# A decoder block: the first head's probabilities turned by the DMA queues and VectorE in place of TensorE

## The chip, the cores and the metric

The kernel runs on one NeuronCore of a Trainium2 chip. The metric is the device time of one execution in microseconds (us); the median of three runs before the change is 3028.91 us (3027.8 to 3032.17).

## The reference, cut to what matters

Sixteen sequences (B = 16) of 512 tokens of width 512 pass four phases: linear attention with a local convolution (A), cross-attention to `ctx_1024` (B), a recurrent gate over the sequence of items (C), and an output layer (D). The change is in B. There each of 4 heads has 128 dimensions and all heads share one key and one value head:

```
q = rope(rmsnorm(x) @ q_w)              # 4 heads, 512 tokens, 128
k, v = rope(mem @ k_w), mem @ v_w       # one head, 512 keys
logits = q @ k.T                        # 4 x 512 x 512
probs = softmax(where(mask, logits, -big))
enc = probs @ v ; out = enc @ out_w
```

All matrix products are made of three passes over operands that are split in a high part (fp32r, rounded) and a low part (the remainder), so that they keep nearly fp32 precision.

## The kernel before, in words

**Pipeline.** In phase B `pipeline3` runs 18 steps s. A step works on three items at once: `new` (item s: keys, values, queries), `old` (item s-1: softmax and the first three heads' products) and `fin` (item s-2: last head and output). Each step has 16 slots j = 0..15, one per softmax tile (head h = j // 4, 128 tokens t = j % 4, all 512 keys). Each engine walks the slots in its own written order and waits on semaphores; nothing is planned at run time. SyncE (SP) issues every DMA, strictly in its written order: a wait of one DMA holds all later ones.

**The life of a softmax tile.** On TensorE `logits(j)` writes one of two PSUM banks. On VectorE `masked(j)` adds the mask row, takes the maximum and writes the tile to `soft`, which has 4 places (so tile j+4 waits until tile j has been read). ScalarE takes `exp`, VectorE `one_over`, GpSimd `normalise` (L1316). TensorE turns the tile, `turn_p(j)` (L1723): four fp32 transposes of 128x128 into one of two banks. ScalarE's `p_high` (L1388) and VectorE's `p_low` (L1539) split the turned tile into `p[h % 2]`; `turn_p(j)` waits for `p_low(j-2)`, since the bank is the same. `encode(h)` multiplies the four turned tiles of a head with v. In slot j an engine works on: logits(j+2), turn_p(j) on TensorE; one_over(j+1), masked(j+2), p_low(j-1) on VectorE, in this order; p_high(j-1), exp(j+2) on ScalarE; normalise(j+1) on GpSimd. `encode(0)` of `old` is in slot 8.

**Other work in the slots.** TensorE: values and keys of `new` in slots 0, 2, 3, the output of `fin` in 4 to 7, the queries of `new` in 9 to 14. VectorE: `tokens_turned(c)`, a transpose in 32x32 squares of the x of `new` (L388), in slots 5 to 8, and `residual` beside it. ScalarE: `tokens_high(c)` (L1416) in 5 to 8 and `memory_high(c)` (L1243), the split of the next item's memory, in 6 to 9; both stand ahead of the next slot's p_high in ScalarE's order. GpSimd: `tokens_low(c)` (L1320) in slots 6 to 8.

**SP's order in a step.** Load the residual of `fin`; `shuffle_x`: wait for the normalised x, store it to DRAM (`out` is used as scratch, L1118), wait until it has landed, and load it back with its 128-column blocks moved (four DMAs of 256 KB in pieces of 512 B, L382); then the next item's mask (L1127), its memory (L1109), its x (L1114), and the store of `fin` (L1302).

Of the kernel before, what the change touches and what calls it, by code (L numbers as in the profile page):

```python
# [7 lines left out]
F32 = mybir.dt.float32  # L8
# [188 lines left out]
class Kernel:  # L197
# [842 lines left out]
    def phase_b(self, ctx):  # L1040
# [5 lines left out]
        SLOTS = 4  # L1046
        with ExitStack() as held:
# [8 lines left out]
            q = self.split(ctx, "b_q", [P, H, S])  # L1056
            p = [self.split(ctx, f"b_p{i}", [P, T, S]) for i in range(2)]
            memT = Split(sb("memT_hi", [P, C, S], F32R), Place(nc, self.base + 1024 * 196).tile("b_memT_lo", [P, C, S], F32R))
# [33 lines left out]
            kv_ps, v_hi, v_lo = ev("kv_ps", 2), ev("v_hi", 2 * T), ev("v_lo", T)  # L1092
            k_rope = ev("k_rope", 8)
            kT_ps, k_hi, k_lo = ev("kT_ps"), ev("k_hi"), ev("k_lo")
            x_moved = ev("x_moved", 5, 16)
            x_turned, xT_hi, xT_lo = ev("x_turned", C), ev("xT_hi", C), ev("xT_lo", C)
            q_ps, q_cos, q_swapped, q_sin, q_rope = ev("q_ps", H), ev("q_cos", H), ev("q_swapped", 2 * H), ev("q_sin", H), ev("q_rope", H)
# [3 lines left out]
            pT_ps, p_hi, p_lo = ev("pT_ps", J), ev("p_hi", J), ev("p_lo", J)  # L1101
# [4 lines left out]
            def load_mem(sp, b):  # L1106
                if b >= 1:
                    sp.wait_ge(kv_ps.sem, kv_ps.upto(b - 1))
                sp.dma_start(memT_f[:, :, :], self.token_rows(self.x2, b)).then_inc(mem_in.sem, mem_in.unit)  # L1109
# [6 lines left out]
            def shuffle_x(sp, b):  # L1116
                sp.wait_ge(N.normed.sem, N.normed.upto(b))
                sp.dma_start(self.token_rows(self.out, b), x[:, :, :]).then_inc(x_moved.sem, x_moved.unit)  # L1118
                sp.wait_ge(x_moved.sem, x_moved.upto(b - 1, 0))
                self.load_shuffled(sp, x, self.out, b, x_moved)  # L1120
# [150 lines left out]

            def sync(sp):
                def step(s, new, old, fin):
                    if fin:
# [13 lines left out]
                    if s == B - 1:  # L1288
                        self.c_parameters(sp)
                        sp.wait_ge(kv_ps.sem, kv_ps.upto(B - 1))  # L1290
# [18 lines left out]
            def gpsimd(pool):  # L1309
                pool.wait_ge(params.sem, params.upto(0))  # L1310

                def step(s, new, old, fin):
# [8 lines left out]

                    def query_sin(b, h):
# [9 lines left out]
                    for j in range(J):  # L1332
                        if old and j < J - 1:
                            normalise(old.b, j + 1)
                        if new and j == J - 1:
                            normalise(new.b, 0)
                        if older_goes_on:
# [36 lines left out]
            def scalar(act):  # L1374
                def step(s, new, old, fin):
# [6 lines left out]
                    def p_high(b, j):  # L1382
                        h, t = divmod(j, T)
                        act.wait_ge(pT_ps.sem, pT_ps.upto(b, j))
# [3 lines left out]
                        act.activation(p[h % 2].high[:, :, t * P:(t + 1) * P], pT_banks[j % 2][:, :].rearrange("p (i s) -> p i s", i=T),  # L1388
                                       ACT.Copy).then_inc(p_hi.sem, p_hi.unit)

# [6 lines left out]
                    def values_high(g):  # L1397
                        act.wait_ge(kv_ps.sem, kv_ps.upto(new.b, g))
# [12 lines left out]
                    def tokens_high(c):  # L1411
                        act.wait_ge(x_turned.sem, x_turned.upto(new.b, c))
                        source = turns.bank(s, OUT + c)[:, :] if new.b == 0 else nT_f[:, c, :]
                        if c == 0 and new.b >= 1:
                            act.wait_ge(q_ps.sem, q_ps.upto(new.b - 1))
                        act.activation(nT.high[:, c, :], source, ACT.Copy).then_inc(xT_hi.sem, xT_hi.unit)  # L1416

                    def keys_high():
                        act.wait_ge(kT_ps.sem, kT_ps.upto(new.b))
                        if new.b >= 2:  # L1420
                            act.wait_ge(logit_ps.sem, logit_ps.upto(new.b - 2))
                        act.activation(k[new.par].high[:, :], turns.bank(s, KT)[:, :], ACT.Copy).then_inc(k_hi.sem, k_hi.unit)

                    def query_swap(h):

                        act.wait_ge(q_ps.sem, q_ps.upto(new.b, h))
# [13 lines left out]
                    for j in range(J):  # L1440
                        if old and j >= 1:
                            p_high(old.b, j - 1)
                        if fin:
# [69 lines left out]
            def vector(dve):  # L1513
                dve.wait_ge(params.sem, params.upto(0))

                def step(s, new, old, fin):
# [5 lines left out]
                    def masked(b, j):  # L1522
# [3 lines left out]
                        if free := earlier(pT_ps, b, j, SLOTS):  # L1526
# [8 lines left out]
                    def p_low(b, j):  # L1535
                        h, t = divmod(j, T)
                        dve.wait_ge(p_hi.sem, p_hi.upto(b, j))
# [14 lines left out]
                    def tokens_turned(c):  # L1552
                        if c == 0:
                            dve.wait_ge(x_moved.sem, x_moved.upto(new.b - 1))
                            dve.wait_ge(q_ps.sem, q_ps.upto(new.b - 1))
# [10 lines left out]
                    def keys(g):  # L1566
# [8 lines left out]
                        if g == 0 and new.b >= 1:  # L1575
                            dve.wait_ge(kT_ps.sem, kT_ps.upto(new.b - 1))
# [923 lines left out]
```

## Time and profile before

| | |
|---|---|
| median of 3 runs | 3028.91 us |
| the profiled execution itself | 3028.35 us |
| its span | 3026.6 us |
| TensorE (PE) busy | 2983.4 us, 99% |
| VectorE / ScalarE / GpSimd busy | 1952.0 / 1295.3 / 919.5 us |
| DMA, mean share of 16 engines | 43.2% |
| TensorE's granted clock, mean | 0.997 |

Phase B takes about 880 to 1815 us of the span; from one step to the next pass 57.22 us. Busy shares are averages; a row of a timeline gives start, duration, engine, line, operation and how often; the brackets give the idle time just before and what ended it.

### The profile page before, as it was taken

The numbers are of one execution on the slowest core, as the hardware profiler recorded it, in microseconds if no ns is written. First come the engines' busy times: TensorE is split into PE (matmuls) and PEld (weight loads), VectorE is DVE, ScalarE is ACT, GpSimd is POOL, SyncE is SP. The second block draws the span as 40 slices with busy tenths as digits, with TensorE's granted clock in tenths as the row PEclk, the third lists the DMA queues.
The fourth block names the chain that finished last, engine by engine and source line by source line (L and its number), as shares of the span: only waits on it lengthen the run. The fifth ranks groups of instructions, "written<-read, shape, count | busy, mean of one in ns | idle before, by whom it ended". The sixth has DMA issues, their size and how long they took to land.

```text
span 3026.6 us, 39400 instructions
## 1 busy us (share of the span) xinstructions
PE 2983.4 (99%) x14628; PEld 2508.4 (83%) x14628; DVE 1952.0 (64%) x4095; ACT 1295.3 (43%) x2511; POOL 919.5 (30%) x681
## 2 busy tenths in 40 slices
PE   7999999999989999999999999999999999999999
PEld 6888888888868888888888878888888888888887
DVE  6888888888878888888888774323333433232455
ACT  4444444444457766767766643211112212112243
POOL 0101010101357877777777720000000000000144
PEclk9999999999999999999999999999999999999999
DMA  7777777777733334344344232111111121111486
GB/s 212 201 203 209 202 215 199 215 198 217 205 105 113 105 107 127 99 113 127 99 114 126 71 125 74 56 54 55 42 42 42 56 55 57 42 28 46 153 290 224
DMA packets 319631, 380.07 MB, mean 126 GB/s; under 512 B 15312, under 2 KB 175056, under 8 KB 319440
## 3 DMA queue, kind: packets, MB, share of 16 engines
q1 hardware_dynamic: 319440, 377.56, 43.2%
q8 instruction: 116, 1.90, 0.3%
q14 instruction: 75, 0.61, 0.1%
HBM read 232.80 MB, written 130.02 MB: 120 GB/s over the span
## 4 chain that ended last, share of the span: by engine, by line
PE 96%; DVE 2%; ACT 1%; issue 1%; DMA 0%; POOL 0%; SPq 0%; DVEq 0%; ACTq 0%; POOLq 0%
PE c_p L132 11%; PE c_p L131 11%; PE c_p L130 11%; PE a_p L130 6%; PE a_p L131 6%; PE a_p L132 6%; PE b_n L130 5%; PE b_n L132 5%; PE b_n L131 5%; PE b_t L1723 3%; PE d_p L131 2%; PE d_p L132 2%; PE d_p L130 2%; PE a_p L1017 2%; PE a_r L131 2%; PE a_r L132 2%
## 5 line engine op out<-in xcount | busy, mean ns | idle before, releaser
L1316 POOL TENSOR_SCALAR b_soft<-b_soft,b_one_in_sum 128x512 f32<-128x512 f32 x256 | 401.2, 1568 | 201.5 <-DVE b_one_in_sum L1520 201.3
L1997 ACT ACTIVATE c_gate<-c_p,c_bias 128x512 f32<-128x512 f32 x180 | 124.2, 690 | 682.6 <-PE c_p L132 682.6
L2027 DVE TENSOR_TENSOR c_gate<-c_gate,c_gate 128x512 f32<-128x512 f32 x64 | 44.2, 691 | 502.7 <-ACT c_gate L1997 502.7
L351 POOL TENSOR_TENSOR kept_scale<-c_ln_ve,minus_half 128x4 f32<-128x4 f32 x16 | 16.1, 1008 | 880.4 <-DVE c_ln_ve L343 880.4
L1531 DVE CUSTOM_DVE_ANT_0 b_soft<-b_l,b_mask_row 128x512 f32<-128x512 f32 x256 | 175.6, 686 | 87.9 <-issue 84.0
L351 POOL TENSOR_TENSOR a_ln_sc<-a_ln_ve,minus_half 128x4 f32<-128x4 f32 x16 | 16.3, 1017 | 629.9 <-DVE a_ln_ve L343 629.9
L1379 ACT ACTIVATE b_soft<-b_soft,b_minus_top 128x512 f32<-128x512 f32 x256 | 184.5, 721 | 44.6 <-DVE b_minus_top L1531 42.6
L649 ACT ACTIVATE a_elu<-a_p 128x512 f32<-128x512 f32 x128 | 75.6, 591 | 287.6 <-PE a_p L132 287.6
L1388 ACT ACTIVATE b_p_hi<-b_t 128x512 fp32r<-128x512 f32 x256 | 151.3, 591 | 109.9 <-PE b_t L1723 109.6
L1539 DVE TENSOR_TENSOR b_p_lo<-b_t,b_p_hi 128x512 fp32r<-128x512 f32 x256 | 175.7, 686 | 16.1 <-ACT b_p_hi L1388 14.3
L1723 PE MATMUL b_t<-ident,b_soft 128*128 128x128 f32 x1024 | 154.5, 273 | 4.9 <-POOL b_soft L1316 4.9
L2221 POOL TENSOR_TENSOR d_x<-d_x,d_y 128x512 f32<-128x512 f32 x60 | 79.8, 1332 | 252.8 <-ACT d_y L2238 252.8
L1723 PEld LDWEIGHTS b_t<-ident,b_soft 128*128 128x128 f32 x1024 | 126.0, 142 | 30.5 <-DVE b_p_lo L1539 6.4
L130 PE MATMUL b_l<-b_k_hi,b_q_hi 128*128 128x512 f32 x256 | 123.2, 481 | 2.0 <-POOL b_q_lo L1328 1.6
L2029 DVE TENSOR_TENSOR c_gate<-c_gate,c_c_f 128x512 f32<-128x512 f32 x64 | 44.3, 692 | 116.3 <-ACT c_gate L1997 116.3
L130 PE MATMUL a_p<-a_Wk_hi,a_xT_hi 128*128 128x512 f32 x256 | 105.3, 411 | 0.7 <-DVE a_Wk_lo L194 0.7
L626 POOL TENSOR_TENSOR a_res<-a_res,a_bp 128x512 f32<-128x512 f32 x64 | 82.3, 1318 | 75.9 <-DMA a_res<-in_x 47.4
L666 ACT ACTIVATE a_z_hi<-a_z_sum 128x512 fp32r<-128x512 f32 x64 | 40.5, 633 | 150.2 <-DVE a_z_sum L848 150.2
L130 PE MATMUL b_n<-b_nT_hi,b_qw_hi 128*128 128x512 f32 x256 | 100.7, 393 | 3.0 <-POOL b_nT_lo L1320 3.0
L130 PE MATMUL b_e<-b_p_hi,b_v_hi 128*128 128x512 f32 x256 | 100.4, 392 | 2.9 <-DVE b_enc_lo L1544 2.9
L132 PE MATMUL b_l<-b_k_hi,b_q_lo 128*128 128x512 f32 x256 | 102.0, 398 | 0.0
L130 PE MATMUL a_r<-a_Wp_hi,a_z_hi 128*128 128x512 f32 x256 | 101.2, 395 | 0.0
(301 smaller groups left out, 9617.6 us busy)
## 6 DMA issues: line engine op xcount, KB each, us to landing
a_mem_moving<-in_ctx SPq DMA_DIRECT2D x64, 256.0 KB, 5.2
a_mem_turned<-in_ctx SPq DMA_DIRECT2D x16, 1024.0 KB, 9.2
x<-a_mem_turned SPq DMA_DIRECT2D x16, 1024.0 KB, 7.8
a_res<-in_x SPq DMA_DIRECT2D x16, 1024.0 KB, 6.4
x<-a_res SPq DMA_DIRECT2D x16, 1024.0 KB, 5.2
b_memT_f<-x SPq DMA_DIRECT2D x16, 1024.0 KB, 7.3
b_x<-x SPq DMA_DIRECT2D x16, 1024.0 KB, 6.1
b_res<-x SPq DMA_DIRECT2D x16, 1024.0 KB, 5.5
```

What stands on the lines that cost most here:

```text
L130: pe.matmul(out, stationary.high, moving.high, start=first, stop=False)
L131: pe.matmul(out, stationary.high, moving.low, start=False, stop=False)
L132: return pe.matmul(out, stationary.low, moving.high, start=False, stop=last)
L626: pool.tensor_tensor(res[:, t, :], res[:, t, :], bp[:, :], ALU.add).then_inc(res_bp.sem, res_bp.unit)
L1316: pool.tensor_scalar(soft[:, at, :], soft[:, at, :], one_in_sum[:, at:at + 1], None, ALU.mult).then_inc(p_norm.sem, p_norm.unit)
L1379: act.activation(soft[:, at, :], soft[:, at, :], ACT.Exp, bias=minus_top[:, at:at + 1], scale=-1.0, accum_out=row_sum[:, at:at + 1]).then_ ...
L1388: act.activation(p[h % 2].high[:, :, t * P:(t + 1) * P], pT_banks[j % 2][:, :].rearrange("p (i s) -> p i s", i=T), ACT.Copy).then_inc(p_hi ...
L1531: dve.tensor_tensor_reduce(out=soft[:, at, :], in0=logit_banks[j % 2][:, :], in1=mask_row[b % 2][:, :], scale=-1.0, scalar=3e38, op0=ALU.a ...
L1539: dve.tensor_tensor(part.low, pT_banks[j % 2][:, :].rearrange("p (i s) -> p i s", i=T), part.high_f32(), ALU.subtract).then_inc(p_lo.sem, ...
L1723: mm = pe.transpose(pT_banks[j % 2][:, i * P:(i + 1) * P], soft[:, tile(old.b, j), i * P:(i + 1) * P], self.ident[:, :])
L1997: act.activation(gate[j % 2][i][:, :], gating.banks[(3 * j + i) % 6][:, :], ACT.Tanh if g == "c" else ACT.Sigmoid, bias=added[:, i, j:j + ...
L2221: pool.tensor_tensor(x[old.par][:, t, :], x[old.par][:, t, :], y[:, t % 2, :], ALU.add).then_inc(out_sb.sem, out_sb.unit)
```

## The change: what it does

The four tiles of head 0 of each item no longer go through TensorE. `turn_p` runs only for j >= 4. In their place:

- `shuffle_p(t)` on SP: wait for `normalise(t)`; store the `soft` tile (256 KB) to DRAM; wait until it has landed; wait until VectorE has turned tile t-1 (there is one buffer, `p_shuffled`); load it back in four DMAs of 64 KB in pieces of 512 B.
- `first_head_turned(t)` on VectorE in slots 3 to 6, after `masked` and `p_low`: one transpose in 32x32 squares, 128x512, into `p0_raw`.
- `first_head_high(t)` on ScalarE and `first_head_low(t)` on GpSimd in slots 4 to 7: the split of the turned tile, read from SBUF. The `p_high` and `p_low` of head 0 (slots 1 to 4) are gone.
- SP's order in a step is now: residual load, shuffle_p(0), store_x, shuffle_p(1), shuffle_x (its four loads), shuffle_p(2), shuffle_p(3), mask, memory, x, store.
- A place of `soft` that held a tile of head 0 is free once its store has landed (`soft_free`): masked(4) to masked(7) wait for the stores of tiles 0 to 3.
- `encode(0)` waits for GpSimd's four low halves.
- Keys and mask row are kept in another order of columns (key i*128+w in column 4w+i), so that the 32x32 squares come out right. For that `turn_p` of the other 12 tiles reads every fourth column (a step of 16 bytes), and the copies of the keys from PSUM and of the mask read their source in steps of 128 elements.
- Several semaphores are merged into one (`kvq_ps`), with the same order.

```diff
+            def shuffle_p(sp, b, t):
+                rows = self.out[b, t * P:(t + 1) * P, :]
+                sp.wait_ge(p_norm.sem, p_norm.upto(b, t))
+                sp.dma_start(rows, soft[:, t, :]).then_inc(p_moved.sem, p_moved.unit)
+                sp.wait_ge(p_moved.sem, p_moved.upto(b, 5 * t))
+                if b >= 1 or t >= 1:
+                    sp.wait_ge(p_lo.sem, p_lo.upto(b - (t == 0), first_turned_at[t - 1]))
+                for a in range(4):
+                    sp.dma_start(p_shuffled[32 * a:32 * (a + 1), 0, :].rearrange("m (g n) -> m g n", n=P),
+                                 rows[:, a * P:(a + 1) * P].rearrange("(g m) n -> m g n", m=32)).then_inc(p_moved.sem, p_moved.unit)
...
+                    if old:
+                        shuffle_p(sp, old.b, 0)
+                    if new and new.b >= 1:
+                        store_x(sp, new.b)
+                    if old:
+                        shuffle_p(sp, old.b, 1)
                     if new and new.b >= 1:
                         shuffle_x(sp, new.b)
+                    if old:
+                        shuffle_p(sp, old.b, 2)
+                        shuffle_p(sp, old.b, 3)
                     if following(new, B):
                         load_mask(sp, new.b + 1)
                         load_mem(sp, new.b + 1)
...
-                        if free := earlier(pT_ps, b, j, SLOTS):
+                        if free := soft_free(b, j):
                             dve.wait_ge(*free)
...
+                    def first_head_turned(t):
+                        dve.wait_ge(p_moved.sem, p_moved.upto(old.b, 5 * t + 4))
+                        if t == 0 and old.b >= 1:
+                            dve.wait_ge(enc_ps.sem, enc_ps.upto(old.b - 1, 2))
+                        blocks = p_shuffled[:, 0, :].rearrange("p (n i) -> p i n", i=T)
+                        dve.transpose(p0_raw[:, :, t * P:(t + 1) * P], blocks).then_inc(p_lo.sem, p_lo.unit)
...
-                            mm = pe.transpose(pT_banks[j % 2][:, i * P:(i + 1) * P], soft[:, tile(old.b, j), i * P:(i + 1) * P], self.ident[:, :])
+                            mm = pe.transpose(pT_banks[j % 2][:, i * P:(i + 1) * P], interleaved(soft[:, tile(old.b, j), :], i, T), self.ident[:, :])
...
-                        if old:
+                        if old and j >= T:
                             turn_p(j)
```

## Rows read from the trace of the kernel before

**Rows 1.** The page: busy time of the engines, and the chain that ended last.
```profile
PE 2983.4 (99%) x14628; PEld 2508.4 (83%) x14628; DVE 1952.0 (64%) x4095; ACT 1295.3 (43%) x2511; POOL 919.5 (30%) x681
...
PE 96%; DVE 2%; ACT 1%; issue 1%; DMA 0%; POOL 0%; SPq 0%; DVEq 0%; ACTq 0%; POOLq 0%
```

**Rows 2.** The chain in order of time (start, us, piece), one turn of a tile.
```profile
1228.70 0.44 PE b_t L1723 x4
```

**Rows 3.** Turns reading every fourth column: chain 846 to 860; weight loads, min/median/max ns.
```profile
851.36 0.47 PE b_n L369 x4
...
L369 PEld LDWEIGHTS b_n<-ident,b_x x16: 196/210/221, 847.8 to 857.9; 128*128 128x128 f32 x16
...
L1723 PEld LDWEIGHTS b_t<-ident,b_soft x1024: 137/140/230, 880.3 to 1785.7; 128*128 128x128 f32 x171
```

**Rows 4.** TensorE's timeline of one step: logits(2), (5), (8), turn_p(6), encode(0).
```profile
1275.67 0.48 PE L130 MATMUL b_l<-b_k_hi,b_q_hi 128*128 128x512 f32 x1
...
1286.11 0.48 PE L130 MATMUL b_l<-b_k_hi,b_q_hi 128*128 128x512 f32 x1
...
1296.43 0.47 PE L130 MATMUL b_l<-b_k_hi,b_q_hi 128*128 128x512 f32 x1
...
1299.94 0.60 PE L1723 MATMUL b_t<-ident,b_soft 128*128 128x128 f32 x4
...
1305.38 0.40 PE L130 MATMUL b_e<-b_p_hi,b_v_hi 128*128 128x512 f32 x1
```

**Rows 5.** VectorE's timeline of the same step: masked(5), masked(6), p_low(4).
```profile
1287.10 0.69 DVE L1531 CUSTOM_DVE_ANT_0 b_soft<-b_l,b_mask_row 128x512 f32<-128x512 f32 x1 [0.61 <-issue]
...
1290.55 0.69 DVE L1531 CUSTOM_DVE_ANT_0 b_soft<-b_l,b_mask_row 128x512 f32<-128x512 f32 x1
...
1294.17 0.69 DVE L1539 TENSOR_TENSOR b_p_lo<-b_t,b_p_hi 128x512 fp32r<-128x512 f32 x1
```

**Rows 6.** The same step: GpSimd's normalise(0) and (1), ScalarE's memory_high(0).
```profile
1276.08 3.11 POOL L1316 TENSOR_SCALAR b_soft<-b_soft,b_one_in_sum 128x512 f32<-128x512 f32 x2
...
1301.00 0.61 ACT L1243 ACTIVATE b_memT_hi<-b_memT_f 128x512 fp32r<-128x512 f32 x1
```

**Rows 7.** SP's timeline of the same step: shuffled x, mask, memory.
```profile
1285.10 1.93 SPq L382 DMA_DIRECT2D b_x<-out  x4
1287.13 0.43 SPq L1127 DMA_DIRECT2D b_mask_u<-in_mask_BxS_bk  x1
1288.50 0.38 SPq L1109 DMA_DIRECT2D b_memT_f<-x  x1
```

**Rows 8.** DMA issues: times, KB each, median us to landing; last line is the mask's.
```profile
b_x<-x SPq DMA_DIRECT2D x16, 1024.0 KB, 6.1
...
out<-b_x SPq DMA_DIRECT2D x15, 1024.0 KB, 4.3
...
b_mask_u<-in_mask_BxS_bk SPq DMA_DIRECT2D x16, 64.0 KB, 5.8
...
out<-d_x SPq DMA_DIRECT2D x4, 256.0 KB, 2.0
...
DMA to landing us min/median/max: 5.2/5.8/8.4
```

**Rows 9.** Groups by line, 1225 to 1680 us: times | busy us, mean ns | idle before.
```profile
L1320 POOL TENSOR_TENSOR b_nT_lo<-b_nT_f,b_nT_hi 128x512 fp32r<-128x512 f32 x32 | 41.5, 1297 | 2.9 <-ACT b_nT_hi L1416 2.9
...
L388 DVE STREAM_TRANSPOSE b_nT_f<-b_x 128x512 f32<-128x512 f32 x32 | 34.8, 1087 | 0.0
...
L1416 ACT ACTIVATE b_nT_hi<-b_nT_f 128x512 fp32r<-128x512 f32 x32 | 20.3, 633 | 64.6 <-DVE b_nT_f L388 64.6
```

**Rows 10.** Windows in the first full step: length, busy PE PEld DVE ACT POOL, PEclk, DMA, GB/s.
```profile
889.00:891.00 2.00, 0.62 (x3) 0.18 (x1) 2.00 (x7) 0.60 (x1) 1.54 (x2) 1.00 1.26 188
...
893.00:895.00 2.00, 1.02 (x4) 0.47 (x3) 1.98 (x4) 0.00 (x0) 1.41 (x1) 0.50 1.05 388
...
897.00:899.00 2.00, 1.43 (x9) 1.06 (x7) 1.85 (x4) 0.11 (x1) 2.00 (x2) 0.56 0.00 0
```

More of the change, by code:

```diff
@@ L1046, in phase_b @@
         SLOTS = 4
+        HEAD = 4
         with ExitStack() as held:
@@ L1056, in phase_b @@
             q = self.split(ctx, "b_q", [P, H, S])
+            p0_at = self.place.offset
             p = [self.split(ctx, f"b_p{i}", [P, T, S]) for i in range(2)]
+            p0_raw = Place(nc, p0_at + 4 * T * S).tile("b_p0_raw", [P, T, S])
+            p_shuffled = Place(nc, self.d_bo_at).tile("b_p_shuffled", [P, 1, S])
             memT = Split(sb("memT_hi", [P, C, S], F32R), Place(nc, self.base + 1024 * 196).tile("b_memT_lo", [P, C, S], F32R))
@@ L1270, in tile, with by_tile, by_column, soft_free @@
                 return (b * J + j) % SLOTS
+            def by_tile(row):
+                return row[:, :].rearrange("p (i w) -> p w i", i=T)
+            def by_column(row):
+                return row[:, :].rearrange("p (w i) -> p w i", i=T)
+            def soft_free(b, j):
+                g = b * J + j - SLOTS
+                if g < 0:
+                    return None
+                item, k = divmod(g, J)
+                if k < T:
+                    return p_moved.sem, p_moved.upto(item, 5 * k)
+                return pT_ps.sem, pT_ps.upto(item, k - T)
             def sync(sp):
@@ L1320, in tokens_low, with first_head_low @@
                         pool.tensor_tensor(nT.low[:, c, :], nT_f[:, c, :], nT[:, c, :].high_f32(), ALU.subtract).then_inc(xT_lo.sem, xT_lo.unit)
+                    def first_head_low(t):
+                        pool.wait_ge(p_hi.sem, p_hi.upto(old.b, high_at[t]))
+                        part = (slice(None), slice(None), slice(t * P, (t + 1) * P))
+                        pool.tensor_tensor(p[0].low[part], p0_raw[part], p[0].high[part].bitcast(F32), ALU.subtract).then_inc(p0_lo.sem, p0_lo.unit)
                     def query_sin(b, h):
@@ L1336, in step @@
                             normalise(new.b, 0)
+                        if old and HEAD <= j < HEAD + T:
+                            first_head_low(j - HEAD)
                         if older_goes_on:
@@ L1389, in p_high, with first_head_high @@
                                        ACT.Copy).then_inc(p_hi.sem, p_hi.unit)
+                    def first_head_high(t):
+                        act.wait_ge(p_lo.sem, p_lo.upto(old.b, first_turned_at[t]))
+                        part = (slice(None), slice(None), slice(t * P, (t + 1) * P))
+                        act.activation(p[0].high[part], p0_raw[part], ACT.Copy).then_inc(p_hi.sem, p_hi.unit)
                     def enc_high(b, h):
@@ L1440, in step @@
                     for j in range(J):
-                        if old and j >= 1:
+                        if old and j >= T + 1:
                             p_high(old.b, j - 1)
+                        if old and HEAD <= j < HEAD + T:
+                            first_head_high(j - HEAD)
                         if fin:
@@ L1585, in keys_low @@
                         dve.wait_ge(k_hi.sem, k_hi.upto(new.b))
-                        dve.tensor_tensor(k[new.par].low[:, :], turns.bank(s, KT)[:, :], k[new.par][:, :].high_f32(), ALU.subtract).then_inc(k_lo.sem, k_lo.unit)
+                        dve.tensor_tensor(by_column(k[new.par].low), by_tile(turns.bank(s, KT)), by_column(k[new.par].high.bitcast(F32)), ALU.subtract).then_inc(k_lo.sem, k_lo.unit)
                     def mask():
@@ L1616, in step @@
                             masked(new.b, j - J + 2)
-                        if old and j >= 1:
+                        if old and j >= T + 1:
                             p_low(old.b, j - 1)
+                        if old and HEAD - 1 <= j < HEAD - 1 + T:
+                            first_head_turned(j - HEAD + 1)
                         if fin and j == 0:
@@ L1730, in encode @@
                             pe.wait_ge(v_lo.sem, v_lo.upto(item.b))
-                            pe.wait_ge(p_lo.sem, p_lo.upto(item.b, h * T + T - 1))
+                            if h == 0:
+                                pe.wait_ge(p0_lo.sem, p0_lo.upto(item.b))
+                            else:
+                                pe.wait_ge(p_lo.sem, p_lo.upto(item.b, low_at[h * T + T - 1]))
                         for i in keys:
```

51 lines of the change are left out of this document (29 added, 22 removed).

## The prediction

> **What bounds the kernel now.** I read the page first: TensorE is busy 99% of the span and makes up 96% of the chain that ended last [rows 1]. Then the chain in order of time inside phase B: products and turns follow one another with no piece of another engine between them, and a turned tile is a piece of 0.44 us, which includes what it costs the matmul behind it [rows 2]. So whatever leaves TensorE's stream in phase B is time won, as long as the stream stays without gaps. Then I read one step on each engine. The reader is to see there by how much the others run ahead of TensorE; that lead is what the change spends.
>
> I count T from logits(2) of slot 0, at 1275.67 [rows 4]. Before the change, logits(8) (slot 6) is at T = 20.8, turn_p(6) at 24.3, encode(0) at 29.7 [rows 4]; masked(6) on VectorE starts at T = 14.9 and p_low(4) at 18.5 [rows 5], so each is some 6 us ahead of its use.
>
> **What is taken off TensorE.** 4 tiles x 16 items = 64 turns x 0.44 us = 28.2 us [rows 2]. In a step that is 1.76 us, all in slots 0 to 3. Without any stall the marks become: logits(5) T = 9.1 (10.44 less three turns), logits(8) 19.0, turn_p(6) 22.5, encode(0) 27.9.
>
> **What the other turns cost more.** The remaining 192 turns read every fourth column. Four such turns stand in the chain as 0.47 us [rows 3] against 0.44 [rows 2]: 192 x 0.03 = 5.8 us, 0.36 in a step. Below it can be nothing; the upper end is the weight load's own difference, 210 against 140 ns [rows 3], fully exposed: 4 x 0.07 x 192 = 54 us. I take 0.03 because rows 3 measure just this pattern between two matmuls. The Trainium skill ("Advanced Engine Details and Errata", Memory Cachelines) says that SBUF lines are 16 bytes and that an access which touches each line only once pays a penalty; four-byte words at a step of 16 bytes do that. The longer load agrees with it, the 0.47 says that most is hidden; by the rule with nothing hidden the sum would be 54 us and no longer 6.
>
> **Small edits.** The copies of the keys and the mask with another order of reading are 3 instructions of 0.4 to 0.7 us in a step, off TensorE's path; at twice their time they stay hidden by the lead of 6 us. VectorE loses four p_low of 0.69 (a like row is in [rows 5]) and gains four transposes of 1.09 [rows 9]: +1.6 us in a step of 57, of which it is idle some 9. ScalarE changes four reads of PSUM into four of 0.63 [rows 9]. GpSimd gains 4 x 1.30 = 5.2 us [rows 9] in slots 4 to 7, where it has gaps. Merged semaphores: nothing. All this work is hidden; were it not, it would be 5 us a step at most.
>
> **What the new waits cost.** This is the term that decides. SP is one queue, and each shuffle_p makes it wait for VectorE. Starting from the rows:
>
> Up to the first turn. normalise(0) ends at T = 2.0 (half of the 3.11 us from T = 0.4, [rows 6]). Store 0 lands 2.0 later [rows 8], T = 4.0; its four loads take 1.93 to issue, as four such DMAs do [rows 7], T = 6.0; store_x lands 4.3 later [rows 8], 10.3; store 1 is behind it in the same queues and lands about 11.2 (a quarter of the bytes more). masked(5) needs logits(5) (9.1 + 1.0, [rows 4, 5]) and now this store: T = 11.2, 0.6 us; first_head_turned(0) 1.0 (pipelined start to start, a little less than the 1.09): it ends at T = 12.9.
>
> Leg 1. Only now may SP issue loads 1 (1.93), then the four x loads (1.93, [rows 7]), then store 2, T = 16.8. Whatever is issued right behind the four x loads lands with them: the mask, 64 KB, takes 5.8 us, from 5.2 to 8.4 [rows 8], where 256 KB alone take 2.0. With 0.5 for the size, store 2 lands at T = 23.1. masked(6) waits for it, then first_head_turned(1): T = 24.7. TensorE stands at logits(8) from 19.0 to 23.7: a gap of 4.7.
>
> Leg 2. loads 2 (1.93), store 3 lands 2.3 after that: 28.9. masked(7) waits for it, and behind masked(7) in VectorE's order stand p_low(4), to T = 30.1, and first_head_turned(2), to 31.1. turn_p(6) needs p_low(4): it moves from 22.5 to 30.1.
>
> Leg 3. loads 3 (1.93), mask 0.43, and the next item's memory is issued at T = 33.5, where before it was at 12.8 [rows 7]. One MB takes 6.1 us (the load of x, [rows 8]): T = 39.6. memory_high(0), which before was at 25.3 [rows 6], holds ScalarE; behind it stand p_high(6) and first_head_high(3) (0.5, 0.5, 0.65), then first_head_low(3) on GpSimd, 1.3 [rows 9]: encode(0) can start at T = 42.6, not 27.9 (28.0 with the slower turns). It is 14.6 us late, and since TensorE is the bound behind slot 8, nothing brings that back.
>
> Clock. In the first full step TensorE is busy only 0.62 of 2 us; its granted clock then reads 0.50, i.e. 1.2 GHz, and returns only after the window at 0.56 [rows 10]. Gaps of 4.7 and 6 us are larger than that one, so I expect a fall behind the last one: if some 5 us of work run at half speed, 2.5 us are lost. The falls inside the legs cost nothing, since TensorE waits there. The Trainium skill ("TensorE: Matmul & The Clock Gate", HAM oscillation) describes the same for a kernel that waits for DMA at each tile: every tile starts at the low clock. Rows 10 agree.
>
> A step: +14.6 + 2.5 - 1.76 + 0.36 = +15.7 us. Fifteen steps have both a new and an old item: +236. The sixteenth has no x and no memory to move; its legs are 4.3 us against slots of 3.9, so between -1.3 and +4; I take 0. Sum: 3028.35 (the profiled execution, 0.56 below the median of 3028.91) + 236 = 3264 us.
>
> The ends of the waits' term: with every landing at its lowest (mask 5.2), DMAs that don't queue behind each other (store 2 lands 2.0 after its issue) and no clock loss, encode(0) is still about 9 us late: +7.6 x 15 = +114, 3142. With landings at 8.4 and two falls of the clock that count, 22 us late: +20.6 x 15 = 3337.
>
> **Rivals.**
> Half the stall. The slots before are shorter by 1.76 us only on TensorE, but VectorE and SP may start their part of a step earlier than I have it, so that the legs overlap. For it: VectorE is idle before 0.61 us at masked(5) [rows 5]. Against: each leg starts with a wait for the turn before, which is in VectorE's slot order. Time: 7 us late, +5.6 x 15 = 3112.
> Not slower: the legs hide. This needs store 2 to have landed when VectorE comes to masked(6) at T = 14, or at the latest so that masked(6) ends before logits(8) at 19.0, and the memory at about T = 25. The deciding point is the way from the first turn to store 2's landing: under about 5.5 us the first gap is gone; rows 7 and 8 give 3.9 + 6.3. Then only the turns count: 3028.35 - 28.2 + 5.8 = 3006.
> Strided loads exposed. No stall but 0.28 us for each of 192 turns: 3028.35 - 28.2 + 54 = 3054. This is what the skill's rule of the lines would give. Against it: 0.47 in rows 3.
> Worse: TensorE's clock stays down for most of a step, and SP's delay passes into the next step's x (its load waits for the last tokens_turned). Then 25 us a step, about 3400.
> That the turns do not leave TensorE at all can be excluded by the code.
>
> **How the numbers follow.** The forecast, 3264, has 0.72; half the stall 0.13; hidden legs 0.08; exposed strides 0.02; worse 0.05. The range 3110 to 3345 holds the forecast with both ends of its legs and nearly all of half the stall; it leaves out the hidden legs, the strides and the worst. A measurement tells about 0.2% (6 us) from no change. Faster: 0.08 (the hidden legs). Same: 0.02 (a small stall that just eats the 22 us). Slower: 0.90.
>
> **What would show it.** In the trace after: 768 transposes L1723-like in place of 1024, 0.47 a tile in the chain; SP's memory load about T = 33 of a step; VectorE idle before masked(6) and masked(7), put down to a DMA; TensorE idle at logits(8), turn_p(6) and encode(0); the step 72 to 73 us long; granted clock below 1.0 in every step. I am wrong if VectorE's two waits are under 2 us, or if a step is 56 us; and wrong in the sizes if the memory load is early and encode(0) waits for something else.

## The result, and the profile after

| | before | after |
|---|---|---|
| median, us | 3029.58 (3027.8 to 3032.17, 4 runs) | 3287.12 (3286.58 to 3288.3, 4 runs) |
| ratio to before | | 1.0848, interval 1.0835 to 1.0861 |
| span of the profiled execution, us | 3026.6 | 3285.2 |
| TensorE's granted clock, mean | 0.997 | 0.961 |

The change costs 257.5 us, 8.5%. The forecast was 3264, with a range of 3110 to 3345.

The page of the kernel after: busy times, the chain that ended last by engine, one group (line, busy us, mean ns, idle before it and its releaser) and the stores of softmax tiles (times, KB, median us to landing).

```profile
PE 3062.1 (93%) x14372; PEld 2546.9 (78%) x14372; DVE 1965.8 (60%) x4095; ACT 1298.3 (40%) x2511; POOL 1005.4 (31%) x745
...
PE 74%; DMA 10%; SPq 4%; DVE 4%; POOL 4%; issue 2%; ACT 2%; DVEq 0%; POOLq 0%; ACTq 0%
...
L1589 DVE MEMSET b_carrier<- 128x1 f32 x256 | 15.1, 59 | 194.1 <-DMA out<-b_soft 193.7
...
out<-b_soft SPq DMA_DIRECT2D x64, 256.0 KB, 3.8
```

In [rows 1] the chain was 96% TensorE and 0% DMA; now it is 74% and 10%. L1589 is the first instruction of `masked`: VectorE stands there for 194 us until a store of a softmax tile has landed.

The waits in phase B after (us in total, times, longest us), the worst of TensorE's and the worst of VectorE's:

```profile
PE b_l L130 <- DVE b_minus_top L1590: 66.6, 14, 6.3
PE b_e L130 <- POOL b_p_lo L1370: 53.9, 14, 5.3
PE b_n L1853 <- DVE b_res L1616: 24.1, 13, 2.2
...
DVE b_carrier L1589 <- DMA out<-b_soft: 160.7, 36, 9.4
```

The first is logits(8), the second encode(0), once in each full step (14 of the 15 lie in this window, 900 to 1900 us). The third, the turn of the keys that waits for VectorE's residual, I had not named.

One step of the kernel after. It begins with logits(2) at 1317.25, which is T = 0. SP's queue:

```profile
1330.65 1.76 SPq L1131 DMA_DIRECT2D b_p_shuffled<-out  x4
1332.45 2.02 SPq L382 DMA_DIRECT2D b_x<-out  x4
1334.51 0.49 SPq L1126 DMA_DIRECT2D out<-b_soft  x1
...
1345.57 0.43 SPq L1126 DMA_DIRECT2D out<-b_soft  x1
...
1352.50 0.43 SPq L1116 DMA_DIRECT2D b_memT_f<-x  x1
```

VectorE in the same step: the first turn, masked(6), masked(7), p_low(4).

```profile
1329.47 1.11 DVE L1606 STREAM_TRANSPOSE b_p_raw<-b_p_shuffled 128x512 f32<-128x512 f32 x1
...
1341.02 0.06 DVE L1589 MEMSET b_carrier<- 128x1 f32 x1 [8.69 <-DMA out<-b_soft]
...
1347.81 0.06 DVE L1589 MEMSET b_carrier<- 128x1 f32 x1 [3.26 <-DMA out<-b_soft]
...
1348.47 0.69 DVE L1598 TENSOR_TENSOR b_p_lo<-b_t,b_p_hi 128x512 fp32r<-128x512 f32 x1
```

ScalarE's memory_high(0), and TensorE: logits(8), turn_p(6), the turn of the keys, encode(0).

```profile
1358.37 0.63 ACT L1263 ACTIVATE b_memT_hi<-b_memT_f 128x512 fp32r<-128x512 f32 x1 [1.01 <-DMA b_memT_f<-x]
```

```profile
1341.81 0.80 PE L130 MATMUL b_l<-b_k_hi,b_q_hi 128*128 128x512 f32 x1 [5.08 <-DVE b_minus_top L1590]
...
1349.36 1.04 PE L1793 MATMUL b_t<-ident,b_soft 128*128 128x128 f32 x4
...
1356.62 0.66 PE L1853 MATMUL b_n<-ident,b_k_f 128*128 128x128 f32 x4 [1.83 <-DVE b_res L1616]
1361.50 0.77 PE L130 MATMUL b_e<-b_p_hi,b_v_hi 128*128 128x512 f32 x1 [3.05 <-POOL b_p_lo L1370]
```

Read it downwards. VectorE ends the first turn at 1330.58; SP then issues four loads, the four loads of x, and store 2 at 1334.51; store 2 is down at 1341.02, masked(6) goes, and TensorE restarts at 1341.81. VectorE waits once more in the same way for store 3, and p_low(4) ends at 1349.16. TensorE does not stand for it: it works at half its clock and comes to turn_p(6) only at 1349.36. Only then does SP come to the memory of the next item.

The windows after (length, busy us of PE, PEld, DVE, ACT, POOL, then PEclk, DMA share, GB/s): before the gap, the stretch behind it, behind encode(0)'s gap, and the rest of the step.

```profile
1330.00:1341.00 11.00, 6.73 (x34) 5.54 (x32) 2.30 (x8) 2.06 (x7) 2.88 (x3) 0.95 0.72 143
1341.00:1346.00 5.00, 3.58 (x8) 2.38 (x9) 3.50 (x11) 1.82 (x4) 1.35 (x1) 0.50 0.15 39
...
1361.00:1366.00 5.00, 4.50 (x11) 3.56 (x12) 3.92 (x9) 2.97 (x7) 4.42 (x4) 0.50 0.00 0
1368.00:1378.00 10.00, 10.00 (x49) 8.39 (x48) 7.45 (x20) 7.47 (x15) 8.21 (x6) 1.00 0.78 286
```

The granted clock is 0.50, the level of 1.2 GHz, behind both gaps, as [rows 10] show it once at the start of phase B. Behind the first it lasts until about 1350, behind the second until about 1367; in the rest of the step the clock is 1.00. Over 14 full steps the first product of encode(0) takes 0.69 to 0.77 us in 12 and 0.47 in two, so in two of them the second fall is missing.

The mean step, by 14 issues of the memory load (910.03 to 1870.76), is 73.9 us; before, by the same count, 57.2.

### The profile page after: what moved, and what is told of

It reads as the page before. It is cut to its first block, busy times and chain, and to the rows that moved or that the text cites. A ratio compares the mean times of both kernels' runs of the same rounds, so it can differ in the third digit from the quotient of the medians.

```text
span 3285.2 us, 39271 instructions
## 1 busy us (share of the span) xinstructions
PE 3062.1 (93%) x14372; PEld 2546.9 (78%) x14372; DVE 1965.8 (60%) x4095; ACT 1298.3 (40%) x2511; POOL 1005.4 (31%) x745
## 4 chain that ended last, share of the span: by engine, by line
PE 74%; DMA 10%; SPq 4%; DVE 4%; POOL 4%; issue 2%; ACT 2%; DVEq 0%; POOLq 0%; ACTq 0%
PE c_p L130 10%; PE c_p L132 10%; PE c_p L131 10%; DMA out<-b_soft 7%; PE a_p L130 5%; PE a_p L131 5%; PE a_p L132 5%; SPq L1131 3%; DMA b_memT_f<-x 3%; PE d_p L132 2%; PE d_p L130 2%; PE d_p L131 2%; PE a_p L1017 2%; PE a_r L959 2%; PE a_r L131 2%
## 5 line engine op out<-in xcount | busy, mean ns | idle before, releaser
L2100 DVE TENSOR_TENSOR c_gate<-c_gate,c_gate 128x512 f32<-128x512 f32 x64 | 44.2, 690 | 502.7 <-ACT c_gate L2070 502.7
L130 PE MATMUL b_e<-b_p_hi,b_v_hi 128*128 128x512 f32 x256 | 115.6, 452 | 61.3 <-POOL b_p_lo L1370 58.2
L1598 DVE TENSOR_TENSOR b_p_lo<-b_t,b_p_hi 128x512 fp32r<-128x512 f32 x192 | 131.9, 687 | 37.1 <-ACT b_p_hi L1440 35.3
L1440 ACT ACTIVATE b_p_hi<-b_t 128x512 fp32r<-128x512 f32 x192 | 112.9, 588 | 94.0 <-PE b_t L1793 93.4
L1793 PE MATMUL b_t<-ident,b_soft 128*128 128x128 f32 x768 | 127.3, 290 | 14.0 <-DVE b_p_lo L1598 7.7
L1589 DVE MEMSET b_carrier<- 128x1 f32 x256 | 15.1, 59 | 194.1 <-DMA out<-b_soft 193.7
L130 PE MATMUL b_n<-b_ow_hi,b_enc_hi 128*128 128x512 f32 x256 | 116.6, 456 | 15.7 <-DVE b_k_swap L1646 8.5
L130 PEld LDWEIGHTS b_e<-b_p_hi,b_v_hi 128*128 128x128 f32 x256 | 55.3, 216 | 82.3 <-issue 66.1
L130 PEld LDWEIGHTS b_l<-b_k_hi,b_q_hi 128*128 128x128 f32 x256 | 53.2, 208 | 80.5 <-DVE b_minus_top L1590 77.9
L131 PE MATMUL b_e<-b_p_lo,b_v_hi 128*128 128x512 f32 x256 | 112.5, 440 | 0.0
L132 PE MATMUL b_e<-b_p_hi,b_v_lo 128*128 128x512 f32 x256 | 111.9, 437 | 0.0
```

Of the source, the lines that this page charges most:

```text
L130: pe.matmul(out, stationary.high, moving.high, start=first, stop=False)
L131: pe.matmul(out, stationary.high, moving.low, start=False, stop=False)
L132: return pe.matmul(out, stationary.low, moving.high, start=False, stop=last)
L1793: mm = pe.transpose(pT_banks[j % 2][:, i * P:(i + 1) * P], interleaved(soft[:, tile(old.b, j), :], i, T), self.ident[:, :])
```

## The experiments

All kernels but e3 rest on the kernel after. The kernel before ran beside each on the same chip, at 3030.38 to 3030.89 us. e2, e7, e10 and e11 move only one tile; they leave out the values of tiles 1 to 3 of head 0. The diffs are cut to what matters.

**e1: store 2 ahead of the four x loads.**

```diff
                         shuffle_p(sp, old.b, 1)
+                        store_p(sp, old.b, 2)
                     if new and new.b >= 1:
                         shuffle_x(sp, new.b)
                     if old:
-                        shuffle_p(sp, old.b, 2)
+                        load_p(sp, old.b, 2)
```

> The changed kernel, but SP issues the store of tile 2 before the four loads of x, not after them (its loads follow after them, as before). My theory (SP's order of DMAs and the queues behind it set the stalls): store 2 then lands about 2.4 us after its issue, near T = 17.6 of a step (T from logits(2)), and not at 23.8; the gap of TensorE at logits(8), 5.1 us, goes; masked(7) still waits for store 3, which is now behind the x loads, until about T = 25.5 (30.6 before); encode(0) starts near 39 and not at 44. 5 us less in each of 15 steps: about 3212 us, 3190 to 3235. Rival A (VectorE and GpSimd have too much work, the waits for stores only show it): same time as the changed kernel, 3287. Rival B (the clock makes most of the loss): under 3 us a step less, above 3240.

Measured 3220.96 us (3218.22 to 3223.71), ratio 1.0627 (1.0607 to 1.0646): 66 us less than after. TensorE's largest waits in phase B are now:

```profile
PE b_e L130 <- POOL b_p_lo L1378: 59.0, 15, 4.9
PE b_t L1801 <- DVE b_p_lo L1606: 48.4, 15, 6.1
```

The 66.6 us of logits(8) have left the list. The place of one issue in SP's order is worth 4.4 us a step; a new wait, turn_p(6) for p_low(4), gives a part back.

**e5: mask and memory ahead of the loads of tile 3.** The memory goes out earlier, and the loads of tile 3 then stand behind its 1 MB.

```diff
-                        shuffle_p(sp, old.b, 3)
+                        store_p(sp, old.b, 3)
                     if following(new, B):
                         load_mask(sp, new.b + 1)
                         load_mem(sp, new.b + 1)
+                    if old:
+                        load_p(sp, old.b, 3)
+                    if following(new, B):
                         load_x(sp, new.b + 1)
```

> The changed kernel, but SP issues the next item's mask and memory right after the store of tile 3, before it waits for VectorE's turn of tile 2 and issues the four loads of tile 3. In the changed kernel the memory is issued at T = 35.3 of a step and ScalarE waits for it until 41.1, then encode(0) starts at 44.2. Theory 1 (the memory load ends leg 3 alone): encode(0) 5 us earlier, 15 x 5 = 75 us less, about 3212. Theory 2, which I hold: the loads of tile 3 now stand behind 1 MB, land near T = 37 instead of 36, and VectorE and ScalarE reach memory_high(0) in slot order at T = 41 anyway: 0 to 2 us a step less, 3255 to 3287. Theory 3 (moving it has a price): above 3287.

Measured 3276.78 us (3275.8 to 3277.77), ratio 1.0814 (1.0795 to 1.0834): 10 us less than after, 0.7 a step, which is theory 2. The same waits as above, in e5:

```profile
PE b_n L1863 <- DVE b_res L1626: 46.2, 13, 5.0
PE b_e L130 <- POOL b_p_lo L1380: 19.2, 14, 6.1
```

So the gap moved and did not go. TensorE waits 35 us less at encode(0), but 22 us more at the turn of the keys just ahead of it, since VectorE now stands 23.1 us, over 14 steps, for the loads of tile 3. In the kernel after ScalarE stands 26.4 us over 14 steps for the memory. Both ways, the memory's and that of tile 3, end nearly together, and leg 3 of the prediction has only the memory's.

**e4: a buffer for each of the four tiles** (in `nT_f`), so that SP no longer waits for VectorE's turn.

```diff
-            p_shuffled = Place(nc, self.d_bo_at).tile("b_p_shuffled", [P, 1, S])
+            p_shuffled = nT_f
...
-                if b >= 1 or t >= 1:
-                    sp.wait_ge(p_lo.sem, p_lo.upto(b - (t == 0), first_turned_at[t - 1]))
+                if t == 0:
+                    sp.wait_ge(kvq_ps.sem, kvq_ps.upto(b, 6))
```

> The changed kernel, but each tile of head 0 has a buffer of its own (the place where the turned x comes later), so SP no longer waits for VectorE's turn of the tile before; the order of the DMAs is as in the changed kernel. My theory (the waits for VectorE in SP's order are part of each leg, the x loads ahead of store 2 the other part): store 2 lands near T = 22 (23.8), store 3 near 26.5 (30.6), the memory is issued near 29 (35.3), encode(0) starts near 38 (44.2): 6 us less in 15 steps, about 3199, 3180 to 3225. Rival (the order behind one another in the queues alone counts, not SP's waits): within 15 us of 3287.

Measured 3170.9 us (3170.52 to 3171.28), ratio 1.0461 (1.0442 to 1.0481): 116 us less than after, more than I expected and outside my range. Taking out SP's wait for VectorE saves more than any other single edit, 7.7 us a step. I had counted 6, from an encode(0) that comes earlier, and had left out the clock: the gap before encode(0) is now 2.15 us in 14 steps, where it was 2.2 to 4.9, and its first product takes 0.47 to 0.49 us in 13 of them, so there is no second fall to half speed, which cost some 2.7 us in 12 of 14 steps. The length of that gap alone does not decide it: in the kernel after a gap of 2.16 us came with the fall, and two of 2.88 and 3.29 came without.

**e6: e1 and e4 together.**

> The store of tile 2 ahead of the x loads (run e1) and a buffer for each tile (run e4) together. If the two causes are apart, the savings add: 3287 - 66 - 116 = 3105 at best. By rows: store 2 lands near T = 16, store 3, behind the x loads, near 23.5, so masked(7) and p_low(4) are 2 us late for turn_p(6), and slots 5 and 6 of VectorE still make encode(0) late by the 3 us that run e2 showed: about 3120, 3090 to 3150. Rival (one cause covers the other: the legs run one after another and the longer one stays): 3160 to 3171, no gain over run e4.

Measured 3143.04 us (3139.36 to 3146.72), ratio 1.0373 (1.0354 to 1.0392). On top of e4, store 2's place gives 28 us, where it gave 66 alone: the two savings overlap, which fits that both shorten the same way.

**e2: one move.** Only tile 0 goes through DRAM; all four turns, high and low halves of head 0 are still made. What is left is the price of everything but most of the traffic.

```diff
                     if old:
                         shuffle_p(sp, old.b, 0)
...
-                        shuffle_p(sp, old.b, 1)
...
-                        shuffle_p(sp, old.b, 2)
-                        shuffle_p(sp, old.b, 3)
```

> The changed kernel with only tile 0 of head 0 moved through DRAM; tiles 1 to 3 are not moved (VectorE turns the buffer of tile 0 again), so the values of those tiles are left out. All instructions of VectorE, ScalarE, GpSimd and TensorE are the same; 15 of 20 DMAs a step are gone, and with them SP's waits. My theory (all of the loss is waits for these DMAs): the step without stalls, 3028.9 - 28.2 (64 turns at 0.44) + 5.8 (192 turns at 0.03 more) = 3006.5, within 5 us. Rival A (the work moved to VectorE and GpSimd costs time itself): above 3029. Rival B (turns that read every fourth column cost their whole longer weight load, 0.28 us each): 3054.

Measured 3064.16 us (3061.68 to 3067.32), ratio 1.011 (1.0096 to 1.0124). I expected 3006, so this is a miss: with 15 of the 20 new DMAs of a step gone the kernel is still slower than before. TensorE's wait that shows it (the timeline of e2):

```profile
1322.80 0.47 PE L130 MATMUL b_e<-b_p_hi,b_v_hi 128*128 128x512 f32 x1 [2.16 <-POOL b_p_lo L1365]
```

encode(0) waits for GpSimd, which no queue holds here: 34.0 us in 15 steps.

**e3: the columns alone.** The kernel before, with the keys and the mask in the other order and all 256 turns reading every fourth column.

```diff
-    pe.transpose(pT_banks[j % 2][:, i * P:(i + 1) * P], soft[:, tile(old.b, j), i * P:(i + 1) * P], self.ident[:, :])
+    pe.transpose(pT_banks[j % 2][:, i * P:(i + 1) * P], interleaved(soft[:, tile(old.b, j), :], i, T), self.ident[:, :])
```

> The kernel before with one part of the change alone: keys and mask row in the other order of columns, and all 256 turns on TensorE reading every fourth column. By rows of the trace (0.47 us a turned tile against 0.44): 256 x 0.03 = +7.7 us, 3037; the turns in the trace of the changed kernel are spaced 0.39 before the next matmul against 0.36, which agrees. Rival (the weight load's 70 ns are exposed, 0.28 us a tile, as the skill's page on memory lines would give): +72 us, 3101. Rival 2 (the copies of the keys from PSUM, read in another order, hold TensorE): more than 10 us and a wait at logits(0) of an item.

Measured 3041.77 us (3040.06 to 3042.27, 6 runs) against 3030.68, ratio 1.0035 (1.0023 to 1.0047): +11 us, 0.04 a tile. The chain of e3 has turns of two lengths:

```profile
1004.81 0.49 PE b_t L1729 x4
1008.75 0.47 PE b_t L1729 x4
```

against 0.44 in [rows 2]. Exposed strides would have cost +72 for 256 turns; that rival is out. TensorE's waits in phase B of e3 have none at the logits, so the copies of the keys do not hold it (rival 2), and turns longer by 0.03 to 0.05 us each give 8 to 13 us by themselves. The Trainium skill ("Advanced Engine Details and Errata", Memory Cachelines) has a penalty for an access that goes to a new line each time. The longer load is there (210 against 140 ns, [rows 3]), but most of it does not reach the chain.

**e7: e2, and VectorE turns x ahead of the head tile** in slots 5 and 6.

```diff
-                        if old and HEAD - 1 <= j < HEAD - 1 + T:
-                            first_head_turned(j - HEAD + 1)
                         if new and new.b >= 1 and 5 <= j <= 8:
...
+                        if old and HEAD - 1 <= j < HEAD - 1 + T:
+                            first_head_turned(j - HEAD + 1)
```

> Run e2 (tiles 1 to 3 of head 0 not moved, their values left out) with one more edit: in slots 5 and 6 VectorE turns the x of the new item before the tile of head 0, not after it. Run e2 took 3064 us where the turns alone would give 3006. Theory 1: there ScalarE's exp(7) and exp(8) stand behind tokens_high, which waits for VectorE's turn of x, which stood behind the new transposes of 1.0 us; each of these slots grew from 3.9 to 4.8 us and encode(0) came 3 us late. Then this order gives back about 2 us a step, 3030 to 3040, and exp no longer waits longer than before. Theory 2 (GpSimd is too slow: normalise(8), 1.57, and the low half of tile 3, 1.3 us, stand in series in front of encode(0), whatever VectorE does): the time stays near 3064, with POOL as what ends TensorE's wait at encode(0).

Measured 3028.33 us (3026.68 to 3030.39, 11 runs) against 3030.38, ratio 0.9996 (0.9987 to 1.0005): 36 us less than e2, and no different from before. So the place of one instruction of 1.1 us was worth 2.4 us a step. In e2 the head tile, turned first, made the turn of x late. This made ScalarE's tokens_high late, which stands ahead of exp in its order: from one tokens_high to the next passed 4.84 us in e2 (1313.37 to 1318.21) and pass 3.88 in e7 (1298.78 to 1302.66). The wait of encode(0) for GpSimd fell from 34.0 to 13.7 us. This is what is left of it, in the chain of e7:

```profile
1300.49 1.56 POOL b_soft L1356
1302.06 1.27 POOL b_p_lo L1365
1303.32 1.26 POOL b_nT_lo L1360
1304.58 1.54 POOL b_soft L1356
1306.13 1.26 POOL b_p_lo L1365
...
1307.52 0.47 PE b_e L130
```

Five operations of GpSimd in series, 6.9 us without a gap, and encode(0) at their end.

**e8: e6 with e7's order of VectorE** (everything moved).

> Run e6 (store 2 ahead of the x loads, a buffer for each tile) with VectorE's order of run e7. If VectorE's serial work in slots 5 and 6 still bounds e6, this is 15 to 40 us less than e6, near 3090. If the waits for store 3 and for the loads of tiles 2 and 3 bound it, it is within 10 us of e6; and if the x loads are what lands last, VectorE now waits for them ahead of the turns and it is slower than e6.

Measured 3130.43 us (3130.2 to 3130.65), ratio 1.0331 (1.0313 to 1.035): 13 us less than e6 (9 to 17 by the single runs), between my two branches and not the 36 of the one-move kernel. With the traffic in place the tiles come later, and VectorE's order matters less.

**e9: e8 with store 3, too, ahead of the x loads**; the loads of tiles 2 and 3 are waited for together.

```diff
                         store_p(sp, old.b, 2)
+                        store_p(sp, old.b, 3)
                     if new and new.b >= 1:
                         shuffle_x(sp, new.b)
```

> Change: four buffers, VectorE turns x first, and the stores of tiles 2 and 3 both ahead of the four x loads (e8 had only store 2 there). Theory A, the queue's order is still what holds the step: store 3, which in e8 is issued at 1340.65 behind six loads and is waited for until 1346.09, lands some 4 us earlier, and with it the loads of tile 3 and the memory; encode(0) comes 1 to 2 us earlier: 3100 to 3118 us. Rival B, what is left is VectorE's and GpSimd's own work in slots 5 to 8 (masked, turn of x, turn of the head tile, low half, normalise in series): then the memory and store 3 are early in the trace, but the step stays, 3125 to 3135 us.

Measured 3097.19 us (3095.57 to 3099.4), ratio 1.0223 (1.0207 to 1.0238): 33 us less than e8, a little more than theory A gave. A step is 61.7 us. TensorE's largest waits in phase B:

```profile
PE b_n L130 <- DVE b_res L1626: 32.9, 14, 3.3
PE b_e L130 <- POOL b_p_lo L1380: 20.4, 16, 2.9
```

The first is the output product, which waits for VectorE's residual. In the chain the last landing is followed by GpSimd again:

```profile
1328.07 5.14 DMA b_nT_f<-out
...
1335.06 1.56 POOL b_soft L1371
1336.62 1.27 POOL b_p_lo L1380
1337.88 1.24 POOL b_nT_lo L1375
```

**e10: e7 with the turns and splits one slot earlier** (`HEAD = 3`, with the tables of counts to match).

> Change: as e7 (only tile 0 is moved through DRAM, the values of tiles 1 to 3 are left out; all of head 0's turns, high and low halves are still made), with the four turns and splits one slot earlier (turns in slots 2 to 5, splits in 3 to 6), so that GpSimd's low(3) stands ahead of normalise(8), not behind it. Theory A: in e7 the wait of encode(0) for GpSimd, 13.7 us in the window of phase B, was all that ate the gain; it goes, and the time is 3030.4 less 28.2 (64 turns of 0.44) plus 11.1 (the column order, measured): 3013 us, 3008 to 3019. Rival B: GpSimd's 5.2 us more in a step hold normalise and so turn_p wherever they stand; the wait moves from encode(0) to turn_p of slots 4 to 7, and the time stays at 3024 to 3032.

Measured 3048.97 us (3047.4 to 3051.09), ratio 1.0062 (1.0049 to 1.0074): 21 us more than e7. Both ranges missed, and theory A fell. Its first half held, the wait of encode(0) for GpSimd is gone; but another came, not at turn_p, where B put it, but at the queries:

```profile
PE b_n L130 <- POOL b_nT_lo L1360: 23.6, 30, 1.5
```

That is 10 us more than the 13.7 of e7; the other 11 of the 21 are not placed. The chain of e10 shows where the wait comes from. It runs through a ring of VectorE and ScalarE in slots 6 and 7:

```profile
1309.89 0.60 DVE b_p_lo L1593
1310.50 1.02 DVE b_nT_f L388
...
1311.54 0.63 ACT b_nT_hi L1468
1312.17 0.71 ACT b_soft L1426 x2
1312.88 0.52 ACT b_memT_hi L1263
1313.40 0.49 ACT b_p_hi L1435
...
1313.91 0.69 DVE b_p_lo L1593
```

From one p_low to the next pass 4.02 us, and the next round (to 1318.04) takes 4.13. Each p_low waits for the p_high that stands behind exp and memory_high, and tokens_high waits for the turn that stands behind p_low. Ahead of this ring the chain is VectorE alone: from logits(4) on, from 1293.60 to 1311.50, it is busy 17.80 of 17.90 us, where before it was busy 15.20 of 17.80 at the same place (1284.40 to 1302.20).

**e11: e10 with memory_high(0) to (2) behind the next slot's p_high.**

```diff
                             first_head_high(j - HEAD)
+                        if after and 7 <= j <= 9:
+                            memory_high(act, after, j - 7)
...
-                        if after and 6 <= j <= 9:
-                            memory_high(act, after, j - 6)
+                        if after and j == 9:
+                            memory_high(act, after, 3)
```

> Change: as e10 (tile 0 alone is moved through DRAM, the values of tiles 1 to 3 are left out), and ScalarE's memory_high(0) to (2) stand behind the next slot's p_high, not ahead of it. In e10's chain of waits slots 5 to 8 are a ring between VectorE and ScalarE: p_low 0.69, turn of x 1.02, tokens_high 0.63, exp 0.71, memory_high 0.52, p_high 0.49: 4.1 us a slot, where TensorE has 3.5 of work in slots 5 and 6. Theory A, this ring is what kept the gain of the 64 turns from coming out: without memory_high it is 3.5 us, the wait of the queries for GpSimd's low halves (23.6 us in all) goes, and the time is 3030.4 - 28.2 + 11.1 = 3013 us, 3008 to 3022. Rival B, another engine's sum over a slot is the limit (GpSimd in slots 7 to 9: 1.57 + 1.3 + 1.3 each): 3035 to 3050, as e10.

Measured 3037.88 us (3037.15 to 3041.68, 8 runs) against 3030.89, ratio 1.0026 (1.0016 to 1.0036): 11 us less than e10, where A said some 36, and within the range of rival B. But B's mechanism, GpSimd's sum over a slot, is not what the chain shows. The ring is shorter, and it now closes through masked:

```profile
1308.90 0.60 DVE b_p_lo L1595
1309.51 1.01 DVE b_nT_f L388
...
1310.54 0.63 ACT b_nT_hi L1468
1311.17 0.71 ACT b_soft L1426 x2
...
1312.08 0.67 DVE b_soft L1587
...
1312.76 0.60 DVE b_p_lo L1595
```

That is 3.86 us a slot, not the 3.5 I had counted: exp, one_over, masked, p_low, turn, tokens_high, exp. TensorE's own slot here is 3.91 (from one turn_p to the next, 1299.47 to 1303.38), so the ring keeps pace with it but hardly makes up a late start. Ahead of the ring the chain is VectorE's here too, without a gap (busy 17.73 of 17.80 us from 1288.80).

**e12: e9 with the same move.**

> Change: as e9 (all data moved, all stores first), with the same move of memory_high. Theory A for this kernel: its chain is the landing of the loads of tile 3 (5.1 us behind seven other loads) and then GpSimd in series (normalise, low half, low half of x, normalise, low half: 6.9 us), neither of which the ring touches; so at most the wait for VectorE's residual (32.9 us in all) shrinks: 3080 to 3098 us. Rival B, the ring is the limit here too: 3060 us or less.

Measured 3097.61 us (3096.16 to 3099.81), ratio 1.0221 (1.0206 to 1.0237): the same as e9, at the upper end of theory A. Where everything is moved, this edit of the ring changes nothing.

No kernel with all of head 0 moved came below the kernel before; the best, e9, is 2.2% above it.

## Why the prediction was right, step by step

| mark, T in us | forecast | after |
|---|---|---|
| first turn ended | 12.9 | 13.3 |
| store 2 landed | 23.1 | 23.8 |
| logits(8), gap before it | 23.7, 4.7 | 24.6, 5.1 |
| store 3 landed | 28.9 | 30.6 |
| turn_p(6) | 30.1, after a wait | 32.1, no wait |
| memory issued | 33.5 | 35.3 |
| memory landed | 39.6 | 41.1 |
| encode(0) | 42.6 | 44.2 |
| mean step | 72.9 | 73.9 |

**The legs.** Each mark is within some 2 us, and the forecast is right by its mechanism: SP's one order, with VectorE's turns and stores that someone waits for in it. The price of a store behind the x loads, taken from the mask's landing in [rows 8], was the term that mattered: 6.3 forecast, 6.4 to 6.5 here (1334.51 to 1341.02), and 5.8 to 6.8 in the steps before it. e1 and e4 show by their savings that both halves of the leg are causes: SP's wait for the turn, and what stands ahead of the store in the queue. In leg 2 the four loads took 2.66 us to issue, not 1.93. Leg 3 had the right mark by one of two ways only: the memory and tile 3's own data arrive nearly together, and e5, which sends the memory first, gives back 0.7 us of it. The Trainium skill ("DMA: Bandwidth & Descriptors", Queues, rings and completion order) says that a semaphore's write lands only after every earlier write of the same DMA engine; in this trace store 2 lands after 6.4 us behind the 1 MB of the x loads, and store 3, which has only four loads of 64 KB ahead of it, after at most 2.2 (1345.57 to 1347.81), which agrees.

**The clock.** 2.5 us a step forecast; behind encode(0)'s gap TensorE runs at 1.2 GHz from 1361.50 to 1366.96, and half of that, 2.7, is lost. That the fall behind logits(8) costs nothing nearly held too: turn_p(6) came 0.2 us after the p_low(4) that it needs and took 0.71 us until the next product, not 0.39. The forecast had TensorE idle there; the slow clock fills that wait.

**The sum.** 15 x (73.9 - 57.2) = 250; the other 7 us of 257.5 are mostly the sixteenth step, which I had put at 0, between -1.3 and +4. From encode(0) of the fifteenth step to the last product with v in phase B pass 95.4 us (1954.4 to 2049.8), where before passed 85.3 (1705.9 to 1791.2); 2.7 of these 10.1 are the clock behind encode(0), counted above, and TensorE waits 4.2 us there for GpSimd's low halves and 2.8 for p_low. Ahead of the first logits of B lies 0.9. The forecast was 23 us too low: 15 from steps that are 1.0 longer, these 7, and 1 from the base.

**The column order.** 5.8 us forecast for 192 turns. e3's 11 us (7 to 14) for 256 are 8 for 192. The chain had 0.47 in one pattern and 0.49 in another; I had read only the first.

**What failed: "All this work is hidden".** I priced the small edits at nothing, with 5 us a step as the end. e2 less (3030.4 - 28.2 + 8) is 54 us, 3.6 a step. 2.4 of it was the place of the head tile's turn ahead of x's (e7); most of the rest is GpSimd, whose new low halves stand in series with normalise and the low halves of x just before encode(0). In the kernel after it hardly shows, as the waits for the queue lie over it, so the forecast was near although this term was wrong; it decides what is left once the traffic is gone. My error was to add up idle time of an engine over a step. What counts is which slot the work is in and what stands behind it in the same engine's order: GpSimd was busy 443 of 570 us in ten steps before (1000 to 1570 us), and 5.2 us more fit into a step's 13 us of idle time; yet in the 6.9 us before encode(0) there is no gap for them. VectorE is the same case: 9 us idle in a step, but in e10 and e11 it is full for nearly 18 us.

**The lever itself.** Had nothing been lost, the gain would be 28 - 8 = 20 us. e7, e10 and e11 take away most of the traffic and order those operations in three ways, and none is faster: e7 cannot be told from the kernel before, e10 and e11 are 18 and 7 us above it. In e10 and e11 the chain has left TensorE: VectorE works without a gap from logits(4) on, and then a ring of VectorE and ScalarE takes 3.9 to 4.1 us a slot. That shortening VectorE's work there would bring the gain is not tested. In the order of the change "hidden legs", 3006, could not have come about even with the queue nearly free, for e2 has that order and takes 3064. Whether another order gets the 20 us is left open.

**Of the loss of 257 us** 190 came back by SP's order and buffers and VectorE's order without moving less data (e6, e8, e9: 144, 13, 33). e9 is still 67 us above before, and as it has saved the 28 us of the turns, 95 have to be found. The output products wait 32.9 us for VectorE's residual, the turn of the keys waits 7.6 for the same, encode(0) waits 20.4 for GpSimd, and the column order is 8: 69 together. The rest is not placed; the lower clock (0.992 against 0.997 in the mean) is part of it.

## What to carry to other kernels

Before work is moved off the busiest engine, write down for each other engine the order of one slot. Add up its own work over a few slots, and the closed ring of waits between two engines; where either is as long as the busiest engine's slots, the freed time may not come out, as in e10 and e11. A wait put into the one queue that issues all DMAs is priced by what stands behind it: taking it out gave 7.7 us a step (e4). Stores that someone waits for belong ahead of big loads that nobody waits for yet: moving one gave 4.4 us a step (e1). And when an edit changes one wait, look at the waits beside it: in e5 35 us less at one place came with 22 us more at another.

## What of the hardware was not expected

- A 256 KB store took 2.0, 3.8 and 6.8 us to land (least, median, most of 64); the most where it was issued right behind four loads of 256 KB in pieces of 512 B.
- The gap before encode(0) can cost more than its own length: in the kernel after the clock was at half behind it in 12 of 14 steps, which loses 2.7 us more in the step shown; in e4, with gaps of 2.15 us, it stayed at full in 13 of 14.
- In e9 eight loads of 64 KB, issued right behind the four of x, are down 5.1 us after the last issue; a load of 64 KB took 2.0 in the median of the kernel after, where four go out together.
- Read at a step of 16 bytes, a weight load takes 210 ns instead of 140, and of the 0.28 us that this is in a tile 0.04 show.
